# The experts' output bias: summed by TensorE at the end of layer 1 in place of by GpSimd in the middle of it

## The chip, the cores and the metric

The kernel runs on one core of one Trainium2 chip. The metric is the device time of one launch in microseconds (us); the median of three runs of the kernel before is 626.78 us (620.87 to 627.47). The five engines of the core run their own instruction queues and meet only at semaphores: TensorE (PE in the profile, with its weight loads as PEld), VectorE (DVE), ScalarE (ACT), GpSimd (POOL) and SyncE (SP, which here only issues transfers).

## The reference, cut to what matters

The input has 16 batches of 256 rows of 128 numbers. The network has an attention layer with 16 heads, then a layer with a second attention (4 heads) and a mixture of 8 experts. Each row goes to the one expert with the highest logit:

```python
idx = jnp.argmax(logits, axis=-1)
for e in range(E):                                   # E = 8, D = 128, DF = 512
    m = (idx == e)[:, None].astype(xf.dtype)
    h = jax.nn.relu(xf @ W1[e] + b1[e])
    out = out + m * (h @ W2[e] + b2[e])
```

The kernel uses relu(a + b1) = max(a, -b1) + b1. So it computes h' = max(x W1[e], -b1[e]) per row, and what is missing, b1[e] W2[e] + b2[e], is a constant row of 128 numbers per expert. These 8 rows, 1024 numbers in all, are **the output bias**, and it depends on the parameters alone. This is the part of the computation that the change moves.

## The kernel before, in words

There are three stages, each one a block of the program that ends with a barrier of all engines: the first layer (`first_layer`, about 0 to 337 us of the profiled span), the second attention with the sorting of rows by expert (`second_attention`, to about 504 us), and the experts (`experts`, to the end). All of it is float32, which TensorE takes as two records per matmul in the profile.

**Layer 1** is a loop over the batches, `iteration(i)` for i up to LAST + 2 = 17, written out by hand on each engine. In iteration i, TensorE makes the scores of batch i (line 226, into `psB`), the scores of batch i + 1 whose row maxima are needed (line 209, into the three banks of `psA`), the products of probabilities and values (`attend`, line 240) and the projections (lines 183 and 191). VectorE reduces each bank of `psA` to its maxima (line 331) and gives it back; the next scores into this bank wait for that (`a_free`). Between these it normalises the heads of the batch before (lines 346, 353 and 355; line 355 multiplies two operands that both lie in SBUF). ScalarE does the exponentials (line 493). GpSimd has per iteration: normalising a batch three ahead (lines 561 to 579), adding the attention's result two behind (lines 561 to 598), and spreading the keys of two ahead (`spread`, line 586, waiting for ScalarE's `kraw`). In iteration 16 only the end of the last batch is left: `attend(15, 3)`, then `project(15)` on TensorE, then VectorE's residual (lines 317 to 305) and GpSimd's `add_attention` (line 598), which raises `x1_ok`. On that, SyncE moves the last batch to `xs` (line 674) and ScalarE writes it to the output (line 535, counted by `kept`); SyncE waits for all moves to `xs` and for `kept` before it goes to the barrier.

**The output bias before.** From iteration 7, after `spread`, GpSimd also does `bias_part(f)` for f = 0 to 3 (line 617: slice f of W2 times the column of b1, 128x1024 numbers, summed over partitions only later), from iteration 8 `bias_sum(f)` (line 626: adds the product to `w["bias"]`), and in iteration 11 `bias_rest` (lines 631 to 633: adds b2 to partition 0, makes -b1 as `nb1T` and a tile of ones). In the experts' stage the matmul in `output` (line 1456) with `ones` as the stationary operand sums `w["bias"]` over the partitions and starts the sum of each tile.

The weights of the experts (`loads`) are fetched on ScalarE's queue in iterations 1 to 5; all users wait on `loaded`.

Of the kernel before, what the change touches and what calls it, by code (L numbers as in the profile page):

```python
# [8 lines left out]
ALU = mybir.AluOpType  # L9
ACT = mybir.ActivationFunctionType  # L10
AX = mybir.AxisListType

P = 128
B1, L1 = 16, 256
# [8 lines left out]
LAST = B1 - 1  # L23
# [8 lines left out]
def first_layer(nc, x, w_qkv, b_qkv, w_o, b_o, ident, identh, minus_half, xs, out, kept, loads2, loaded2, w, loads,  # L32
                loaded):

    with ExitStack() as ctx:
# [6 lines left out]
        def sem(name):  # L42
# [39 lines left out]
        psA = pb("psA", [P, 3, 512])  # L82
# [5 lines left out]
                 "m_step", "w_ok", "stats0", "stats1", "aggr0", "aggr1", "ln0_step", "ln1_step", "xn_ok", "xnb_ok",  # L88
                 "full", "free", "q_ok", "k_ok", "km_ok", "v_ok", "v_zero", "a_full", "a_free",
                 "turned", "norm_ok", "heads_ok", "onT_ok", "mrow0", "mrow1", "b_full", "b_free", "av_done", "o_ev", "rden_ok", "x1_ok", "stored",  # L90
                 "part_ok", "bias_ok"]
        S = {n: sem(n) for n in names}

        x_t = x.rearrange("b (p c) d -> p b c d", p=P)
# [53 lines left out]
        def _(pe):  # L148
            T = nc.tensor
# [95 lines left out]
            def project(b):  # L245
                pe.wait_ge(S["onT_ok"], b + 1)
                begin("out", b)
                token_major(onT, 1)

            def iteration(i):  # L250
                here, next_, done = fits(i, 0), fits(i, 1), fits(i, -1)
                for g in range(8):
                    if next_:
                        scores_for_max(i + 1, 2 * g)
                        scores_for_max(i + 1, 2 * g + 1)
                    if here and next_:
                        scores(i, 2 * g)
                        scores(i, 2 * g + 1)
                    if here and not next_ and g % 2 == 0:
                        for h in range(2 * g, 2 * g + 4):  # L260
                            scores(i, h)
                    if here and g in (3, 5, 7):
                        attend(i, g // 2 - 1)
                    if g == 0 and i >= 2 and here:
                        prep_v(i)
                    if g == 1 and done:
                        attend(i - 1, 3)
                    if g == 1 and fits(i, 2):
                        prep_x(i + 2)
                    if g in (2, 4) and fits(i, 2):  # L270
                        prep_qk(i + 2, g // 2 - 1, 0)
                        prep_qk(i + 2, g // 2 - 1, 1)
                    if g == 6 and done:
                        project(i - 1)

            pe.wait_ge(S["w_ok"], 5)
            prep_x(0)
# [154 lines left out]
        def _(act):  # L432
# [96 lines left out]
            for i in range(LAST + 2):  # L529
                if 1 <= i <= 5:  # L530
                    for to, source in loads[2 * i - 2:2 * i]:
                        act.dma_start(to, source, allow_slow_non_contiguous=True).then_inc(loaded, 16)
                iteration(i)
            act.wait_ge(S["x1_ok"], B1)
            act.dma_start(out[LAST * L1:B1 * L1, :].rearrange("(p c) d -> p c d", p=P),
                          x_all[:, 2 * LAST:2 * B1, :]).then_inc(kept, 16)
# [3 lines left out]
        def _(pool):  # L540
# [66 lines left out]
                if fits(i, 2):  # L607
                    spread(i + 2)

            b1_of = w["b1T"][:, :].rearrange("p (e f) -> p e f", f=NF)  # L610

            def bias_part(f):

                to = w["part"] if f else w["bias"]
                pool.wait_ge(loaded, 16 * len(loads))
                pool.wait_ge(S["bias_ok"], f)
                G.tensor_tensor(to[:, :].rearrange("p (e d) -> p e d", d=P),
                                w["w2"][:, f, :].rearrange("p (e d) -> p e d", d=P),
                                b1_of[:, :, f:f + 1].broadcast_to([P, NE, P]), ALU.mult
                                ).then_inc(S["part_ok" if f else "bias_ok"], 1)  # L620

            def bias_sum(f):

                pool.wait_ge(S["part_ok"], f)
                pool.wait_ge(S["bias_ok"], f)
                G.tensor_tensor(w["bias"][:, :], w["bias"][:, :], w["part"][:, :], ALU.add).then_inc(S["bias_ok"], 1)

            def bias_rest():

                pool.wait_ge(S["bias_ok"], NF)  # L630
                G.tensor_tensor(w["bias"][0:1, :], w["bias"][0:1, :], w["b2r"][:, :], ALU.add)
                G.tensor_scalar(w["nb1T"][:, :], w["b1T"][:, :], -1.0, None, ALU.mult)
                G.memset(w["ones"][:, :], 1.0)

            norm_x(0)
            norm_x(1)
# [10 lines left out]
            G.tensor_copy(identh[:, :], ident[:, :])  # L647
            for i in range(LAST + 3):
                iteration(i)
                if 7 <= i < 7 + NF:  # L650
                    bias_part(i - 7)
                if 7 < i < 7 + NF:
                    bias_sum(i - 7)
                if i == 7 + NF:
                    bias_rest()


        @block.sync
# [704 lines left out]
def expert_weights(nc, ctx, w):  # L1363

    W1, b1, W2, b2, g2, be2 = w
    t = {"w1": [P, NE * DF], "w2": [P, NF, NE * P], "b2r": [1, NE * P], "g2r": [P, P], "be2r": [P, P],
         "nb1T": [P, NE * NF], "b1T": [P, NE * NF], "bias": [P, NE * P], "part": [P, NE * P], "ones": [P, P]}
    t = {name: ctx.enter_context(nc.sbuf_tensor("e_" + name, shape, F32)) for name, shape in t.items()}
    loads = [(t["w1"][:, :].rearrange("p (e f) -> p e f", f=DF), W1.rearrange("e d f -> d e f"))]
    loads += [(t["w2"][:, f, :].rearrange("p (e d) -> p e d", d=P),  # L1370
               W2[:, f * P:(f + 1) * P, :].rearrange("e p d -> p e d")) for f in range(NF)]
    loads += [(t["b1T"][:, :], b1.rearrange("e (f p) -> p (e f)", p=P)),
              (t["b2r"][:, :], b2.rearrange("(o e) d -> o (e d)", o=1)),
              (t["g2r"][:, :], g2.partition_broadcast(P)), (t["be2r"][:, :], be2.partition_broadcast(P))]
    return t, loads


def experts(nc, w, ident, kept, sorting, sent, padded, y_sorted, out):

    with ExitStack() as ctx:  # L1380
        def sb(name, shape, dt=F32):
# [2 lines left out]
        def pb(name):  # L1384
# [18 lines left out]

        names = ["consts", "t_full", "yT_ok", "own_ok", "h_full", "h_ok", "o_full", "z0_ok", "st0", "st1", "mv0",
                 "mv1", "sd0", "sd1", "inv0", "inv1", "rs0", "rs1", "z1_ok", "z2_step", "z2_ok", "w_ok"]
        names += [f"ys{r}" for r in range(RING)] + [f"put{r}" for r in range(WRING)]
        S = {n: ctx.enter_context(nc.semaphore("ex_" + n)) for n in names}

        w1_i, w2_i, b1_i, row_i = sorting

# [17 lines left out]
        @block.tensor  # L1428
        def _(pe):
            T = nc.tensor  # L1430

            def turn(t):
                pe.wait_ge(S[f"ys{t % RING}"], 16 * (t // RING + 1))
                if t >= 2:
                    pe.wait_ge(S["yT_ok"], t - 1)
                T.transpose(psT[t % 2][:, 0:P], ys[:, t % RING, 0:P], ident[:, :]).then_inc(S["t_full"], 1)

            def hidden(t):
                pe.wait_ge(S["yT_ok"], t + 1)
                pe.wait_ge(S["own_ok"], t + 1)  # L1440
                if t >= 2:
                    pe.wait_ge(S["h_ok"], t - 1)
                for f in range(NF):
                    last = T.matmul(psH[t % 2][:, f * P:(f + 1) * P], own[:, t % 3, f * P:(f + 1) * P],  # L1444
                                    yT[:, t % 3, :], start=True, stop=True)
                last.then_inc(S["h_full"], 1)

            def output(t):
                g = group(t)
                k = t - FIRST[g]  # L1450
                e = pe.value_load(w2_i[0:1, t:t + 1], min_val=0, max_val=(NE - 1) * P)
                pe.wait_ge(S["h_ok"], t + 1)
                if k == 0 and g >= 2:
                    pe.wait_ge(S["z0_ok"], g - 1)
                to = psO[g % 2][:, k * P:(k + 1) * P]
                T.matmul(to, w["ones"][:, :], w["bias"][:, bass.ds(e, P)], start=True, stop=False)
                for f in range(NF):
                    last = T.matmul(to, hT[:, t % 2, f, :], w["w2"][:, f, bass.ds(e, P)], start=False,  # L1458
                                    stop=(f == NF - 1))
                last.then_inc(S["o_full"], 1)  # L1460

            turn(0)
            turn(1)
            for t in range(NS + 1):
                if t < NS:
                    hidden(t)
                if t + 2 < NS:
                    turn(t + 2)
                if t >= 1:
                    output(t - 1)  # L1470
# [179 lines left out]
def build_program(nc, a, out):  # L1650
    with ExitStack() as ctx:
# [3 lines left out]
        xs = ctx.enter_context(nc.sbuf_tensor("xs", [P, NT, P], F32))  # L1655
        y_sorted = nc.dram_tensor("y_sorted", (LAST_ROW, YROW), F32).ap()
        kept = ctx.enter_context(nc.semaphore("kept"))
        loaded2 = ctx.enter_context(nc.semaphore("loaded2"))
        parameters, loads2 = attention_parameters(nc, ctx, [a[k] for k in ("Wqkv", "bqkv", "Wo", "bo", "g1", "be1",
                                                                           "Wg")])  # L1660
# [12 lines left out]
                   for name, n in (("w1_i", NS), ("w2_i", NS), ("b1_i", NS), ("row_i", NS))]  # L1673
# [4 lines left out]
        second_attention(nc, parameters, loaded2, loads2, ident, identh,  # L1678
                         minus_half, xs, y_all, logits, w, loaded, loads, y_sorted, slots, slot_i, base, sorting, sent, zeros,
                         pad_i, padded)  # L1680
        experts(nc, w, ident, kept, sorting, sent, padded, y_sorted, out)


# [21 lines left out]
```

## Time and profile before

| | |
|---|---|
| median of the runs shown | 626.78 us (626.78, 627.47, 620.87) |
| span of the profiled execution, first to last instruction | 624.8 us |
| its own device time | not given with the profile; the median lies 2.0 us above its span |
| PE busy | 524.8 us, 84% of the span |
| DVE busy | 448.6 us, 72% |
| ACT busy | 358.2 us, 57% |
| POOL busy | 314.3 us, 50% |
| one full iteration of layer 1, spread to spread | 16.93 us, three of them 18.40 to 19.98 |
| mean granted TensorE clock | 0.905 of full |

A share of busy time is a mean over three stages that have different limits. In layer 1 TensorE is busy nearly all the time, so the length of an iteration there says more than the shares: it is read from one `spread` (line 586) to the next.

### The profile page before, as it was taken

How to read it: one execution, taken by the hardware profiler on the slowest of the kernel's cores; microseconds unless marked ns; L12 is line 12 of the kernel's file. 1: busy time of each engine (PE TensorE's matmuls, PEld its weight loads, DVE VectorE, ACT ScalarE, POOL GpSimd, SP SyncE). 2: the span in 40 equal slices, each digit the busy share in tenths (PEclk: the TensorE clock that was granted, in tenths of full speed). 3: DMA queues.
4: the chain of work that ended last, by engine and by line, in shares of the span. 5: the costliest groups of instructions: out<-in, count | busy, mean ns of one | idle time of the engine just before them, and what ended most of it. 6: DMA issues, size and time to landing. Idle time of an engine off the chain costs nothing. (4 is left out here: it accounts for less than half of the span.)

```text
span 624.8 us, 15886 instructions
## 1 busy us (share of the span) xinstructions
PE 524.8 (84%) x5168; PEld 383.2 (61%) x5168; DVE 448.6 (72%) x1274; ACT 358.2 (57%) x969; POOL 314.3 (50%) x523
## 2 busy tenths in 40 slices
PE   2899999999999999999972899999957249999910
PEld 2576666666666565666641677677736249999910
DVE  2255878888888888888842789998685626888860
ACT  1214567676676656677560688876653025767760
POOL 5140244433445567422133638887884610477776
PEclk9999999999999988999995899997775559999965
DMA  4300523111011100101111000000001122244333
GB/s 98 87 2 2 170 71 38 24 23 20 19 20 19 21 19 3 20 19 20 20 36 34 35 2 2 2 3 10 20 31 38 59 77 68 34 60 64 32 33 31
DMA packets 38099, 21.62 MB, mean 35 GB/s; under 512 B 13433, under 2 KB 36353, under 8 KB 38018
## 3 DMA queue, kind: packets, MB, share of 16 engines
q1 hardware_dynamic: 18544, 10.65, 7.6%
q0 software_dynamic: 6640, 4.92, 5.6%
q10 hardware_dynamic: 12834, 5.04, 3.2%
q8 instruction: 43, 0.70, 0.5%
q14 instruction: 38, 0.31, 0.2%
HBM read 10.11 MB, written 8.12 MB: 29 GB/s over the span
## 5 line engine op out<-in xcount | busy, mean ns | idle before, releaser
L331 DVE TENSOR_REDUCE nmax<-psA 128x2 f32<-128x512 f32 x256 | 164.9, 685 | 63.7 <-PE psA L209 63.1
L493 ACT ACTIVATE pr<-psB 128x512 f32<-128x512 f32 x250 | 136.0, 595 | 95.1 <-PE psB L226 94.9
L209 PE MATMUL psA<-km,qp 24*128 24x256 f32 x768 | 128.9, 432 | 2.2 <-DVE nmax L331 1.7
L226 PE MATMUL psB<-q,km 26*128 26x256 f32 (+1 forms) x752 | 112.6, 416 | 0.2 <-DMA q<-mT 0.2
L209 PEld LDWEIGHTS psA<-km,qp 24*128 24x128 f32 x768 | 81.2, 200 | 34.8 <-DVE nmax L331 22.6
L1627 POOL DMA_INDIRECT out<-wz,ys x39 | 63.3, 1624 | 53.0 <-ACT wz L1582 44.1
L586 POOL TENSOR_TENSOR km<-kraw,rows_of 128x768 f32<-128x768 f32 x16 | 23.5, 1467 | 122.7 <-ACT kraw L468 115.1
L226 PEld LDWEIGHTS psB<-q,km 26*128 26x128 f32 (+1 forms) x752 | 70.0, 191 | 1.3 <-DMA q<-mT 0.6
L240 PE MATMUL psO<-pr,v 128*32 128x256 f32 x1024 | 70.3, 393 | 0.1
L1180 ACT ACTIVATE prob<-psS,nbias 128x128 f32<-128x128 f32 x128 | 45.6, 386 | 7.0 <-DVE nbias L998 7.0
L240 PEld LDWEIGHTS psO<-pr,v 128*32 128x32 f32 x1024 | 27.2, 111 | 33.8 <-issue 22.5
L1483 DVE TENSOR_TENSOR hT<-psH,e_nb1T 128x512 f32<-128x512 f32 x39 | 27.0, 692 | 25.3 <-PE psH L1444 17.8
L183 PE MATMUL misc<-xnT,wqk 128*128 128x256 f32 x128 | 40.5, 444 | 3.2 <-ACT xnT L442 1.9
L1444 PE MATMUL psH<-yT,own 128*128 128x128 f32 x312 | 42.9, 282 | 0.0
L209 PE MATMUL psA<-kraw,qp 8*128 8x256 f32 x256 | 42.7, 416 | 0.0
L1296 POOL DMA_INDIRECT y_sorted<-y_all,slot_i x32 | 32.4, 1014 | 17.7 <-DVE slot_i L1047 9.9
L1458 PE MATMUL psO<-e_w,hT 128*128 x312 | 41.2, 275 | 0.0
L1444 PEld LDWEIGHTS psH<-yT,own 128*128 128x128 f32 x312 | 39.7, 199 | 0.0
L1458 PEld LDWEIGHTS psO<-e_w,hT 128*128 128x128 f32 x312 | 38.0, 192 | 0.0
L1565 ACT ACTIVATE own<-e_w 128x512 f32 x39 | 24.3, 623 | 23.5 <-PEq L752 18.1
L226 PE MATMUL psB<-q,kraw 27*128 27x256 f32 x248 | 36.0, 400 | 0.0
L183 PEld LDWEIGHTS misc<-xnT,wqk 128*128 128x128 f32 x128 | 24.2, 210 | 18.0 <-ACTq L452 6.8
(201 smaller groups left out, 1113.5 us busy)
## 6 DMA issues: line engine op xcount, KB each, us to landing
q<-mT SPq DMA_DIRECT2D x256, 1.0 KB
ys<-y_sorted SPq DMA_DIRECT2D x39, 72.0 KB, 1.9
e_w<-W ACTq DMA_DIRECT2D x1, 2048.0 KB
e_w<-W ACTq DMA_DIRECT2D x4, 512.0 KB
xs<-x_all SPq DMA_DIRECT2D x16, 128.0 KB
out<-x_all SPq DMA_DIRECT2D x15, 128.0 KB, 3.8
x_all<-x SPq DMA_DIRECT2D x1, 1536.0 KB, 8.9
out<-wz,ys POOLq DMA_INDIRECT x39, 3.3
```

What stands on the lines that cost most here:

```text
L183: made = T.matmul(misc[:, t * L1:(t + 1) * L1], wqk[:, k, t, :], xnT[:, b % 2, :], start=True, stop=True)
L209: last = T.matmul(psA[:, (16 * b + n) % 3, c * L1:(c + 1) * L1], query_part(b, h, depth, c), keys(b, h, depth, slice(0, L1)), start=True, ...
L226: last = T.matmul(bank_of(b, h)[:, c * L1:(c + 1) * L1], keys(b, h, depth, slice(c * P, (c + 1) * P)), queries(b, h, depth, slice(0, L1)), ...
L240: last = T.matmul(psO[32 * j:32 * j + 32, (quad % 2) * L1:(quad % 2 + 1) * L1], v32[:, b % SLOTS, c, 4 * quad + j, :], pr[:, (4 * quad + j ...
L331: V.tensor_reduce(nmax[:, b % 2, hf, :, at], psA[:, (16 * b + n) % 3, :].rearrange("p (c m) -> p c m", c=2), AX.X, ALU.max, negate=True).t ...
L493: A.activation(pr[:, h % PRING, :, :].rearrange("p c l -> p (c l)"), bank_of(b, h), ACT.Exp, scale=SCALE1).then_inc(S["b_free"], 1)
L1180: A.activation(prob[:, n, c, h, :], psS[s][:, u * P:(u + 1) * P], ACT.Exp, bias=nbias[:, s, u:u + 1], scale=SCALE2, accum_out=den[:, n, c, ...
L1296: G.indirect_dma_start(y_sorted, bass.IndirectOffsetOnAxis(slot_i[:, j:j + 1], 0), y_all[:, j, :], None).then_inc(sent, 16)
L1444: last = T.matmul(psH[t % 2][:, f * P:(f + 1) * P], own[:, t % 3, f * P:(f + 1) * P], yT[:, t % 3, :], start=True, stop=True)
L1458: last = T.matmul(to, hT[:, t % 2, f, :], w["w2"][:, f, bass.ds(e, P)], start=False, stop=(f == NF - 1))
L1483: V.tensor_tensor(hT[:, t % 2, :, :], psH[t % 2][:, :].rearrange("p (f n) -> p f n", f=NF), w["nb1T"][:, bass.ds(e, NF)].unsqueeze(2).broa ...
L1627: G.indirect_dma_start(out, bass.IndirectOffsetOnAxis(ids[:, t % RING, P:P + 1], 0), wz[:, t % WRING, :], None, compute_op=ALU.add).then_i ...
```

## The change

The products and sums on GpSimd are taken out; `expert_constants`, in iteration 7, keeps -b1 and the ones. TensorE makes the bias in iteration 16 of layer 1, in two groups of four experts, into two banks of `psA`, which by then no one else uses. The first group stands in its queue between `attend(15, 3)` and `project(15)`, the second behind `project(15)`. Each group is one matmul with one row (ones times b2, 512 columns) and 16 matmuls of 128 columns whose stationary operand is one column of b1, repeated 128 times, and whose moving operand is a slice of W2. So each of the 128 partitions of the result holds the whole bias row. ScalarE copies the two banks to `w["bias"]`, ahead of its wait for `x1_ok` and the last output. In the experts' stage the matmul that starts a tile's sum has the identity in place of the ones as the stationary operand. The tile `part` goes, and the eight semaphores `put` are made before the stages in place of within the last one.

```diff
+            def expert_bias(j):
+                pe.wait_ge(loaded, 16 * len(loads))
+                pe.wait_ge(S["ones_ok"], 1)
+                pe.wait_ge(S["a_free"], 16 * B1)
+                half = NE // 2
+                T.matmul(psA[:, j, :], w["ones"][0:1, :], w["b2r"][0:1, j * half * P:(j + 1) * half * P], start=True,
+                         stop=False)
+                for k in range(half):
+                    e = j * half + k
+                    for f in range(NF):
+                        last = T.matmul(psA[:, j, k * P:(k + 1) * P],
+                                        w["b1T"][:, e * NF + f:e * NF + f + 1].broadcast_to([P, P]),
+                                        w["w2"][:, f, e * P:(e + 1) * P], start=False,
+                                        stop=(k == half - 1 and f == NF - 1))
+                last.then_inc(S["bias_full"], 1)
...
                     if g == 6 and done:
                         project(i - 1)
+                    if i == LAST + 1 and g in (1, 6):
+                        expert_bias(g // 6)
...
                 iteration(i)
+            for j in range(2):
+                act.wait_ge(S["bias_full"], j + 1)
+                A.activation(w["bias"][:, j * 512:(j + 1) * 512], psA[:, j, :], ACT.Copy)
             act.wait_ge(S["x1_ok"], B1)
             act.dma_start(out[LAST * L1:B1 * L1, :].rearrange("(p c) d -> p c d", p=P),
...
-            def bias_part(f):
-                to = w["part"] if f else w["bias"]
...
-                G.tensor_tensor(to[:, :].rearrange("p (e d) -> p e d", d=P),
-                                w["w2"][:, f, :].rearrange("p (e d) -> p e d", d=P),
-                                b1_of[:, :, f:f + 1].broadcast_to([P, NE, P]), ALU.mult
-                                ).then_inc(S["part_ok" if f else "bias_ok"], 1)
-            def bias_sum(f):
...
-                G.tensor_tensor(w["bias"][:, :], w["bias"][:, :], w["part"][:, :], ALU.add).then_inc(S["bias_ok"], 1)
-            def bias_rest():
-                pool.wait_ge(S["bias_ok"], NF)
-                G.tensor_tensor(w["bias"][0:1, :], w["bias"][0:1, :], w["b2r"][:, :], ALU.add)
+            def expert_constants():
+                pool.wait_ge(loaded, 16 * len(loads))
                 G.tensor_scalar(w["nb1T"][:, :], w["b1T"][:, :], -1.0, None, ALU.mult)
-                G.memset(w["ones"][:, :], 1.0)
+                G.memset(w["ones"][:, :], 1.0).then_inc(S["ones_ok"], 1)
...
                 iteration(i)
-                if 7 <= i < 7 + NF:
-                    bias_part(i - 7)
-                if 7 < i < 7 + NF:
-                    bias_sum(i - 7)
-                if i == 7 + NF:
-                    bias_rest()
+                if i == 7:
+                    expert_constants()
...
-                T.matmul(to, w["ones"][:, :], w["bias"][:, bass.ds(e, P)], start=True, stop=False)
+                T.matmul(to, ident[:, :], w["bias"][:, bass.ds(e, P)], start=True, stop=False)
```

## Rows read from the trace of the kernel before

**Rows 1.** The page: its first line.
```profile
span 624.8 us, 15886 instructions
```

**Rows 2.** Windows from spread to spread: length, busy PE PEld DVE ACT POOL, clock, DMA.
```profile
182.13:199.06 16.93, 16.91 (x214) 10.71 (x210) 13.99 (x30) 11.87 (x25) 8.95 (x14) 1.00 0.10 19
199.06:217.46 18.40, 17.99 (x214) 11.32 (x210) 15.87 (x30) 11.87 (x25) 11.19 (x15) 1.00 0.09 18
217.46:237.41 19.95, 19.54 (x214) 12.05 (x210) 15.98 (x30) 11.87 (x25) 11.19 (x16) 0.91 0.08 15
237.41:257.39 19.98, 19.57 (x214) 11.87 (x210) 15.97 (x30) 11.87 (x25) 11.18 (x16) 0.91 0.08 16
257.39:274.32 16.93, 16.91 (x214) 10.71 (x210) 13.99 (x30) 11.87 (x25) 9.84 (x16) 1.00 0.10 19
```

**Rows 3.** POOL's sums: least/median/most ns, first to last start; then timeline: start, us.
```profile
L626 POOL TENSOR_TENSOR e_bias<-e_bias,e_part x3: 2360/2360/2364, 202.5 to 240.8; 128x1024 f32<-128x1024 f32 x3
...
258.81 2.33 POOL L631 TENSOR_TENSOR e_bias<-e_bias,e_b2r 1x1024 f32<-1x1024 f32 x1
261.13 0.43 POOL L632 TENSOR_SCALAR e_nb1T<-e_b1T 128x32 f32<-128x32 f32 x1
261.52 0.20 POOL L633 MEMSET e_ones<- 128x128 f32 x1
```

**Rows 4.** DVE's line 355, the same way; then the first and last long one.
```profile
L355 DVE TENSOR_TENSOR on<-oT,rden x32: 291/293/2207, 66.0 to 326.4; 128x128 f32<-128x128 f32 x32
...
202.78 2.21 DVE L355 TENSOR_TENSOR on<-oT,rden 128x128 f32<-128x128 f32 x1
...
241.13 2.21 DVE L355 TENSOR_TENSOR on<-oT,rden 128x128 f32<-128x128 f32 x1
```

**Rows 5.** Timeline over the end of layer 1; in brackets idle before and releaser.
```profile
322.50 0.71 PE L191 MATMUL misc<-wvo,onT 128*128 128x128 f32 x4
323.14 2.20 PE L240 MATMUL psO<-pr,v 128*32 128x256 f32 x32
...
327.93 1.01 PE L191 MATMUL misc<-wvo,onT 128*128 128x128 f32 x4 [2.59 <-ACT onT L487]
328.98 0.42 DVE L317 TENSOR_TENSOR r<-misc,xnb_all 128x256 f32<-128x256 f32 x1 [1.64 <-PE misc L191]
...
333.28 0.60 SPq L674 DMA_DIRECT2D xs<-x_all  x1
333.28 0.36 ACTq L535 DMA_DIRECT2D out<-x_all  x1
```

**Rows 6.** SP's wait at the barrier, and when it passed.
```profile
SPq L35 <- DMA xs<-x_all: 2.4, 1, 2.4
...
L35 SPq COMPARE_BRANCH  x1: 38/38/38, 337.5 to 337.5; - x1
```

**Rows 7.** The page's DMA issues: the last output, us to landing at the end.
```profile
out<-x_all ACTq DMA_DIRECT2D x1, 128.0 KB, 1.7
```

**Rows 8.** Timeline of PE in the experts' stage: four matmuls, and what follows.
```profile
522.12 1.06 PE L1444 MATMUL psH<-yT,own 128*128 128x128 f32 x8
523.02 0.27 PE L1436 MATMUL psT<-ident,ys 128*128 128x128 f32 x1
```

**Rows 9.** Timeline of PE at the start of layer 2.
```profile
342.25 2.07 PE L870 MATMUL psQK<-xy,uT 128*128 128x256 f32 x4 [0.47 <-ACT xy L1218]
344.11 1.06 PE L878 MATMUL psVO<-uT,xy 128*128 128x128 f32 x4
...
345.97 1.13 PE L870 MATMUL psQK<-xy,uT 128*128 128x256 f32 x4 [0.47 <-ACT xy L1218]
```

**Rows 10.** Timeline of ACT: a copy of 128x512 numbers from PSUM.
```profile
339.30 0.60 ACT L1172 ACTIVATE uT<-psS 128x512 f32<-128x512 f32 x1 [11.42 <-PE psS L849]
```

**Rows 11.** Windows, PE alone: length, busy (records), granted clock, DMA share, GB/s.
```profile
327.00:328.20 1.20, 0.27 (x2) 1.00 0.00 0
328.20:337.00 8.80, 0.74 (x4) 0.50 0.27 60
```

More of the change, by code:

```diff
@@ L90, in first_layer @@
                  "turned", "norm_ok", "heads_ok", "onT_ok", "mrow0", "mrow1", "b_full", "b_free", "av_done", "o_ev", "rden_ok", "x1_ok", "stored",
-                 "part_ok", "bias_ok"]
+                 "bias_full", "ones_ok"]
         S = {n: sem(n) for n in names}
@@ L608, in iteration @@
                     spread(i + 2)
-            b1_of = w["b1T"][:, :].rearrange("p (e f) -> p e f", f=NF)
-            def bias_part(f):
-                to = w["part"] if f else w["bias"]
+            def expert_constants():
                 pool.wait_ge(loaded, 16 * len(loads))
-                pool.wait_ge(S["bias_ok"], f)
-                G.tensor_tensor(to[:, :].rearrange("p (e d) -> p e d", d=P),
-                                w["w2"][:, f, :].rearrange("p (e d) -> p e d", d=P),
-                                b1_of[:, :, f:f + 1].broadcast_to([P, NE, P]), ALU.mult
-                                ).then_inc(S["part_ok" if f else "bias_ok"], 1)
-            def bias_sum(f):
-                pool.wait_ge(S["part_ok"], f)
-                pool.wait_ge(S["bias_ok"], f)
-                G.tensor_tensor(w["bias"][:, :], w["bias"][:, :], w["part"][:, :], ALU.add).then_inc(S["bias_ok"], 1)
-            def bias_rest():
-                pool.wait_ge(S["bias_ok"], NF)
-                G.tensor_tensor(w["bias"][0:1, :], w["bias"][0:1, :], w["b2r"][:, :], ALU.add)
                 G.tensor_scalar(w["nb1T"][:, :], w["b1T"][:, :], -1.0, None, ALU.mult)
-                G.memset(w["ones"][:, :], 1.0)
+                G.memset(w["ones"][:, :], 1.0).then_inc(S["ones_ok"], 1)
             norm_x(0)
@@ L1366, in expert_weights @@
     t = {"w1": [P, NE * DF], "w2": [P, NF, NE * P], "b2r": [1, NE * P], "g2r": [P, P], "be2r": [P, P],
-         "nb1T": [P, NE * NF], "b1T": [P, NE * NF], "bias": [P, NE * P], "part": [P, NE * P], "ones": [P, P]}
+         "nb1T": [P, NE * NF], "b1T": [P, NE * NF], "bias": [P, NE * P], "ones": [P, P]}
     t = {name: ctx.enter_context(nc.sbuf_tensor("e_" + name, shape, F32)) for name, shape in t.items()}
@@ L1375, in expert_weights, with experts @@
     return t, loads
-def experts(nc, w, ident, kept, sorting, sent, padded, y_sorted, out):
+def experts(nc, w, ident, kept, sorting, sent, padded, y_sorted, out, puts):
     with ExitStack() as ctx:
@@ L1405, in experts @@
                  "mv1", "sd0", "sd1", "inv0", "inv1", "rs0", "rs1", "z1_ok", "z2_step", "z2_ok", "w_ok"]
-        names += [f"ys{r}" for r in range(RING)] + [f"put{r}" for r in range(WRING)]
+        names += [f"ys{r}" for r in range(RING)]
         S = {n: ctx.enter_context(nc.semaphore("ex_" + n)) for n in names}
+        S |= {f"put{r}": puts[r] for r in range(WRING)}
         w1_i, w2_i, b1_i, row_i = sorting
@@ L1657, in build_program @@
         kept = ctx.enter_context(nc.semaphore("kept"))
+        puts = [ctx.enter_context(nc.semaphore(f"put{r}")) for r in range(WRING)]
         loaded2 = ctx.enter_context(nc.semaphore("loaded2"))
@@ L1680, in build_program @@
                          pad_i, padded)
-        experts(nc, w, ident, kept, sorting, sent, padded, y_sorted, out)
+        experts(nc, w, ident, kept, sorting, sent, padded, y_sorted, out, puts)
 def kernel(L0_attn_x, L0_attn_w_qkv, L0_attn_b_qkv, L0_attn_w_o, L0_attn_b_o, L0_ffn_Wqkv, L0_ffn_bqkv, L0_ffn_Wo,
```

## The prediction

> **What bounds the kernel now.** The first views, the page's span of 624.8 us [rows 1] and its busy shares, mislead here: GpSimd is the least busy of the four computing engines and TensorE the busiest, so taking work from the one and giving it to the other looks like a loss. But a share is a mean over three stages, and the change lies in layer 1 alone. So I read that stage iteration by iteration, in windows from one spread of the keys to the next [rows 2]. A plain iteration takes 16.93 us, with TensorE busy for 16.91 of them: TensorE is the bound there, and whatever makes it wait adds to the time. Three iterations take 18.40, 19.95 and 19.98 us with the same 214 TensorE records. They are the three in which GpSimd makes a running sum of the bias (three sums of 2.36 us, from 202.48 to 240.8 [rows 3]).
>
> The timeline says how. VectorE's product of heads and reciprocals, line 355, has a median of 0.29 us over 32 and a longest of 2.21 us [rows 4]. Three are that long, the first at 202.78, the last at 241.13: each starts 0.3 us into a sum (202.5 and 240.8 [rows 3]) and ends about 0.15 us behind its end. So three times VectorE stands for 1.92 us behind GpSimd. The row maxima of the next scores come late, and TensorE, which needs their PSUM bank back, waits: it is busy for 17.99 of the 18.40 us [rows 2]. The first such iteration loses 1.47 us (1.92 less 0.45 that was slack). The other two lose 3.02 and 3.05: there the granted clock of TensorE was 0.91 over the iteration against 1.00 in the others [rows 2], that is, after the pause it went for some us to the lower of its two levels (1.2 in place of 2.4 GHz), which is the further 1.55 to 1.58.
>
> **What is removed.** The three sums: 1.47 + 3.02 + 3.05 = 7.54 us on the path. The products cost nothing: the first of them, in the iteration from 182.13, and the last part, the addition of b2 (2.33 us at 258.81 [rows 3]), stand in iterations of 16.93 us [rows 2]. Taking them away gives nothing.
>
> **What stays on GpSimd.** The negated b1 and the ones, 0.43 + 0.20 = 0.63 us [rows 3], move to iteration 7. The work behind them there, the normalising of a batch three ahead, starts 0.63 us later than in a plain iteration and may touch line 355 for a moment; the first 0.45 us of such a touch was slack above. I cost it at 0. Without that slack it is 0.5 us once.
>
> **What is added at the end of layer 1.** The path there [rows 5]: the last attend (the second half of the 32 records from 323.14) ends at about 325.3; VectorE and ScalarE turn its result; the last projection runs at 327.93 for 1.01 us; the residual follows at 328.98; the two last transfers are issued at 333.28. SyncE passes its wait for the move to `xs` at 337.5 and with that the barrier opens [rows 6]. The last output, issued by ScalarE at the same moment, has landed 1.7 us later, at 335.0 [rows 7], so that branch has 2.5 us to spare.
>
> TensorE idles from 325.3 to 327.93, and the first bias group goes in there. Let T be the time of a group: 16 matmuls of 128 columns and one of 512, which I count as 4 more, so 20. For one of 128 columns I take the experts' stage, where four with a new stationary operand each take from 522.12 to 523.02, 0.89 us, or 0.2225 each [rows 8]: it is the nearest row, a stream of the same shape. T = 20 x 0.2225 = 4.45 us. The projection then starts at 325.3 + 4.45 = 329.75, 1.82 late; but it follows busy TensorE, and at the full clock the same four records take 0.71, not 1.01 [rows 5], so what hangs on it is late by 1.82 - 0.30 = 1.5 us. The move to `xs` and the barrier are late by as much.
>
> The second group runs behind the projection, from 330.4 to 334.85. ScalarE copies the first bank in its idle time and the second, 0.60 us [rows 10], to 335.5; only then comes its wait for the last batch (now 334.8) and the last output, which lands 1.7 later, at 337.2. The move to `xs` lands at 337.5 + 1.5 = 339.0. So the second group and the copies cost nothing as long as that cover of 1.8 us holds; each us of T above it counts twice on this branch.
>
> Bounds of T. No row shows a stationary operand that is one column repeated. Below: 4.45 as taken; a lower end would need a faster stream than any row has. Above, at the full clock: the projection's four records, loads not hidden, take 0.64 to the next (322.50 to 323.14 [rows 5]), 0.32 a matmul, T = 6.4: the projection is late by 3.5, the last output would land at 341.05 and `xs` at 341.0, so the end is late by 3.5. At the lower clock: two matmuls of 256 columns take 342.25 to 344.11 [rows 9], 0.465 per 128 columns, T = 9.3.
>
> **Edits at nothing.** Identity for ones in the experts' stage: same shape, same records. No DMA is added or moved except the last output, above. TensorE's new waits (weights loaded, ones made, `psA` free) are met long before 325. The tile taken out and the place of the semaphores move addresses only.
>
> **The sum.** Span 624.8 [rows 1] - 7.54 + 1.5 = 618.7. The profile doesn't give its own device time; the median of 626.78 lies 2.0 above its span, and with the same 2.0 I get **620.7 us**, 6.1 or 1.0% below.
>
> **Rivals.**
>
> *Slow groups, full clock* (T = 6.4): end late by 3.5, so 622.7. For it: the projection's own rows; against: the experts' stream hides its loads [rows 8].
>
> *Layer 2 starts at the higher clock.* Before, TensorE goes to the lower level at 328.2, after 1.2 us with 0.27 busy [rows 11], and stays there past the barrier, to about 345: of two equal pairs of line 870 the first takes 2.07 us, the second 1.13 [rows 9, 11]. With the groups it is busy to 334.85. If the higher level lasts into layer 2, its first steps shrink: that pair by 0.94, the other few, by my estimate from it, together about as much, so 1.9 us less: 618.8. Against it: the idle stretch to the barrier is still some 4 us, longer than the one after which the clock fell before. The Trainium skill (TensorE: Matmul & The Clock Gate, Part 1) calls the lower clock the default and says activity releases it; by that the new matmuls hold the clock in their own stretch, and the idle stretch behind them takes it away again.
>
> *The work was hidden anyway.* GpSimd is off the chain, its sums stay without effect on the time, and the long iterations have another cause. Then the change only adds its 1.5: 628.3. Against it: three sums, three long products, three long iterations, at the same times. The Trainium skill (Perfetto Trace Analysis, Identifying the Most-Contended Engine) says to improve the engine with the highest occupancy; by that the change helps the wrong engine and burdens the right one. The rows go against it in this stage.
>
> *The second group holds the last output.* If the matmuls run at the lower clock (T = 9.3), the projection starts at 334.6, the second group ends at 344.8, the copy at 345.4, and the last output lands at 347.1: the end is 9.6 late, more than the 7.54 won, and the time is 628.9. It decides from 325.3 + 2T + 0.7 + 0.6 + 1.7 = 337.5 + 7.54 on, T = 8.4. Against it: the clock is full at 327 to 328.2 [rows 11], and TensorE now works there.
>
> **How the numbers follow.** Forecast 0.57, slow groups 0.18, higher clock in layer 2 0.12, hidden anyway 0.04, second group 0.04, others 0.05. About 1% (6.3 us, below 620.5) is what can be told from no change, and my forecast lies at that bound: half of its chance (how often the clock falls after a pause may differ from one execution to the next, and two falls are worth 3.1 us of the 7.54), nearly all of the higher clock and little else make faster 0.42; slower by over 1% needs a T of 11.5 or something I have not seen, 0.03; within 0.55. The range takes in the higher clock and the slow groups, each with some 2 to 3 us for the scatter of the runs shown (6.6 us from lowest to highest): 616 to 625.
>
> **What would show it.** Line 355 never above some 0.6 us; the iterations from 199 on all 16.9; granted clock 1.00 to the end of layer 1; a group of 17 matmuls in 4.4 to 4.5 us from 325.3 - 7.5 on, the projection right behind it; SyncE still released by the move to `xs`, not by the last output. I am wrong if another product of VectorE stands as long behind GpSimd, if a group takes over 6.4 us, or if ScalarE's copy ends after the last batch by more than 2.5 us.

## The result and the profile after

The changed kernel takes 621.29 us (median of 20 runs, 619.92 to 625.67) against 626.73 for the kernel before in the same rounds (20 runs, 620.87 to 629.04). The ratio is 0.9936, 95% interval 0.9918 to 0.9954: 0.6% faster, or 4.0 us by the ratio (the means lie 4.1 us apart, the medians 5.4), where 6.1 us were forecast. In its profiled execution the span is 621.5 us and the device time 623.28, so what lies around the span is 1.8 us here. Over its 20 runs it is 1.7 to 3.1 us, with a mean of 2.2; in 33 runs of the kernel before it is 1.7 to 1.8 each time. So some 0.45 us of what the change gives is lost around the span, where no profile looks.

The first view is again the windows from spread to spread, now of the kernel after, iterations 7 to 10 (length, busy PE, PEld, DVE, ACT, POOL, granted clock, DMA):

```profile
181.58:198.52 16.94, 16.92 (x214) 10.71 (x210) 14.00 (x30) 11.89 (x25) 7.55 (x16) 1.00 0.10 19
198.52:215.45 16.93, 16.91 (x214) 10.71 (x210) 14.00 (x30) 11.90 (x25) 6.98 (x14) 1.00 0.10 19
215.45:232.38 16.93, 16.91 (x214) 10.71 (x210) 13.99 (x30) 11.89 (x25) 6.98 (x13) 1.00 0.09 18
232.38:249.31 16.93, 16.91 (x214) 10.71 (x210) 13.99 (x30) 11.89 (x25) 6.98 (x13) 1.00 0.10 19
```

The three long iterations [rows 2] are gone and the clock is full in each. The product of VectorE (line 355 before, line 374 now; shortest, median and longest in ns):

```profile
L374 DVE TENSOR_TENSOR on<-oT,rden x32: 291/293/615, 66.0 to 318.4; 128x128 f32<-128x128 f32 x32
```

Its longest is 0.62 us in place of 2.21 [rows 4]. Now the end of layer 1, TensorE's timeline (start, duration, line) with ScalarE's row that makes the projection's input, which answers to [rows 5]:

```profile
315.06 2.21 PE L240 MATMUL psO<-pr,v 128*32 128x256 f32 x32
317.19 1.12 PE L256 MATMUL psA<-e_b2r,e_ones 1*128 1x512 f32 x2
318.24 3.84 PE L261 MATMUL psA<-e_w,e_b1T 128*128 128x128 f32 x32
319.29 0.51 ACT L506 ACTIVATE onT<-onR,b_cols 128x256 f32<-128x256 f32 x1 [3.16 <-DVE onR L383]
321.92 0.61 PE L191 MATMUL misc<-wvo,onT 128*128 128x128 f32 x4
322.46 1.12 PE L256 MATMUL psA<-e_b2r,e_ones 1*128 1x512 f32 x2
```

The first group runs from 317.19 to the projection at 321.92, 4.7 us; the projection's input was made by 319.8, so it starts 2.1 us late. SyncE's waits there, and the page's row of the last output (us to landing at its end), against [rows 6, 7]:

```profile
SPq L713 <- DMA out<-x_all: 3.8, 1, 3.8
SPq L35 <- PEq L35: 0.2, 1, 0.2
```
```profile
out<-x_all ACTq DMA_DIRECT2D x1, 128.0 KB, 3.9
```

This is new: SyncE now waits for the last output, which takes 3.9 us to land in place of 1.7.

All kernels have the same layers 2 and 3 but for one operand, so I cut each profile at three points: the start of the spread of iteration 8, the first matmul of layer 2, and the first copy of the experts' stage. The first stretch holds the three sums and the end of layer 1; how long layer 1 takes to get there is left out (197.3 to 200.9 us in the profiles of this document, the nine more sums apart, with no order among the kernels).

| | iteration 8 to layer 2 | layer 2 | experts | span |
|---|---|---|---|---|
| before | 138.86 | 167.42 | 119.44 | 624.8 |
| after | 133.28 | 170.62 | 119.12 | 621.5 |

Layer 1 gives 5.6 us in these two profiles, and layer 2 takes 3.2 us of it back. Whether the change does that, and how much of the 7.54 us is there in other executions, is what the experiments are for.

### The profile page after: what moved, and what is told of

Same layout as the page of the kernel before. It is cut to its first block and busy times, and to the rows that moved or that the text cites. A ratio compares the mean times of both kernels' runs of the same rounds, so it can differ in the third digit from the quotient of the medians.

```text
span 621.5 us, 16011 instructions
## 1 busy us (share of the span) xinstructions
PE 529.1 (85%) x5236; PEld 389.6 (63%) x5236; DVE 441.6 (71%) x1274; ACT 360.3 (58%) x971; POOL 298.0 (48%) x515
## 3 DMA queue, kind: packets, MB, share of 16 engines
q0 software_dynamic: 6640, 4.92, 5.6%
## 5 line engine op out<-in xcount | busy, mean ns | idle before, releaser
L209 PE MATMUL psA<-km,qp 24*128 24x256 f32 x768 | 124.5, 427 | 1.0 <-POOL km L608 0.5
L226 PE MATMUL psB<-q,km 26*128 26x256 f32 (+1 forms) x752 | 111.0, 411 | 0.0
L209 PEld LDWEIGHTS psA<-km,qp 24*128 24x128 f32 x768 | 79.2, 198 | 32.1 <-DVE nmax L350 20.5
L240 PE MATMUL psO<-pr,v 128*32 128x256 f32 x1024 | 68.8, 386 | 0.1
L583 POOL TENSOR_SCALAR ve<-mv_r 128x2 f32<-128x2 f32 x16 | 3.8, 237 | 76.2 <-DVE mv_r L324 76.2
```

Source lines behind the costliest of these rows:

```text
L209: last = T.matmul(psA[:, (16 * b + n) % 3, c * L1:(c + 1) * L1], query_part(b, h, depth, c), keys(b, h, depth, slice(0, L1)), start=True, ...
L226: last = T.matmul(bank_of(b, h)[:, c * L1:(c + 1) * L1], keys(b, h, depth, slice(c * P, (c + 1) * P)), queries(b, h, depth, slice(0, L1)), ...
L240: last = T.matmul(psO[32 * j:32 * j + 32, (quad % 2) * L1:(quad % 2 + 1) * L1], v32[:, b % SLOTS, c, 4 * quad + j, :], pr[:, (4 * quad + j ...
```

## The experiments

In what follows a stall is an iteration in which line 355 stands behind a sum, and a fall is TensorE's clock going to its lower level after it. My theory: VectorE's product stands behind GpSimd's sum because both read SBUF; each stall costs 1.47 us, and the clock's falls and layer 2's length go with the execution. Rivals: the amount of GpSimd's work is what delays layer 1; the falls belong to the stall; the bias matmuls cost layer 2 something.

**The sums later in GpSimd's queue.** The kernel before, with `bias_sum` taken from behind the spread and put into the next iteration:

```diff
                     add_bo(i + 3)
+                if 8 < i < 8 + NF:
+                    bias_sum(i - 8)
                 if fits(i, -2):
...
-                if 7 < i < 7 + NF:
-                    bias_sum(i - 7)
```

> The kernel before with the same sums on GpSimd, only later in its queue: each sum stands between adding the output bias of the attention (line 579 of before) and add_attention of the next iteration, where no product of line 355 falls. Theory (the sum holds VectorE's two-input product up): line 355 stays at 0.3 to 0.6 us, every iteration from 131 us on takes 16.93 us, layer 1 ends about 7.5 us earlier than in the profile of before (first matmul of layer 2 at 330.4), with nothing to pay at its end; the time is 1 to 2 us below the changed kernel. Rival (GpSimd's amount of work is what delays layer 1): GpSimd has the same work, the three iterations stay at 18.4 to 20 us and the time stays at that of before.

619.26 us (6 runs, ratio 0.989, interval 0.9857 to 0.9923). Its windows of the same three iterations:

```profile
199.90:216.83 16.93, 16.91 (x214) 10.71 (x210) 13.99 (x30) 11.87 (x25) 11.27 (x15) 1.00 0.10 19
216.83:233.77 16.94, 16.92 (x214) 10.71 (x210) 14.00 (x30) 11.87 (x25) 11.27 (x16) 1.00 0.10 18
233.77:250.70 16.93, 16.91 (x214) 10.71 (x210) 13.99 (x30) 11.87 (x25) 11.26 (x15) 1.00 0.10 19
```

GpSimd is as busy as before (11.27 against 11.19 us [rows 2]), and the stall is gone. The place of the sums was the cause, not the amount of work. Nothing is paid at the end: 131.03 us from iteration 8 to layer 2. (Layer 2 starts at 330.93 and not at 330.4, since iteration 8 starts 0.84 us later than in the first profile of before.)

**The changed kernel again**, unchanged.

> The changed kernel unchanged. In its first profile layer 1 was 6.1 us shorter than before (first matmul of layer 2 at 331.8 against 337.9), but layer 2 (to the first copy of the experts' stage) took 170.6 us against 167.4. Theory: the length of layer 2 goes with where TensorE's clock falls in one execution and not with the change, so this profile gives some other length, within 166 to 172; layer 1 again ends at 331.8 +- 0.3. Rival (the bias matmuls cost layer 2 its clock at the start): 170 to 171 again, with the second pair of 256-column matmuls in layer 2 still slow.

622.07 us (12 runs, ratio 0.994, 0.9918 to 0.9962). From iteration 8 to layer 2 133.24 us, as in the first profile; layer 2 167.32 in place of 170.62. So those 3.2 us belonged to that execution. (Layer 2 starts at 332.52, outside the 331.8 +- 0.3 that I had expected, since iteration 8 starts 0.76 us later here.) The first matmuls of layer 2 in this profile show where the clock was:

```profile
332.52 0.63 PE L847 MATMUL psS<-ident,u_nat 128*128 128x128 f32 x4 [4.41 <-PEq L35]
...
336.85 2.07 PE L869 MATMUL psQK<-xy,uT 128*128 128x256 f32 x4 [0.47 <-ACT xy L1217]
...
340.68 1.13 PE L869 MATMUL psQK<-xy,uT 128*128 128x256 f32 x4 [0.47 <-ACT xy L1217]
```

The transposes take 0.63 us (1.08 in the first profile of after), at the higher level (granted clock 1.00); the first pair of line 869 is back at the lower one (0.50), as in [rows 9].

**The kernel before again**, unchanged, twice.

> The kernel before unchanged. Theory: in each execution the three products wait 1.92 us, but the clock falls after only some of the pauses, so layer 1 ends between 334.8 (no fall) and 339.5 (three); layer 2 between 166 and 172. Rival (the clock falls are part of the stall): 337.9 again with the two falls at the same places, and layer 2 at 167.4.

> The kernel before, a third profile, to count falls of the clock: so far two, one and none... of three pauses fell (two in the first profile, one in the second; one of twelve with more sums). Theory (the falls go with the execution): between none and three of the three iterations at 20 us, the others at 18.4. Rival (two of three as a rule): 19.9 to 20 us twice.

625.19 and 628.15 us, one run each. Their windows of the three iterations, the second profile and then the third:

```profile
199.32:219.36 20.04, 19.62 (x214) 12.06 (x210) 15.99 (x30) 11.88 (x25) 11.22 (x15) 0.91 0.09 16
219.36:237.77 18.41, 17.99 (x214) 11.32 (x210) 15.89 (x30) 11.89 (x25) 11.22 (x16) 1.00 0.09 17
237.77:256.18 18.41, 17.99 (x214) 11.32 (x210) 15.89 (x30) 11.88 (x25) 11.21 (x15) 1.00 0.09 17
```
```profile
199.78:218.18 18.40, 17.99 (x214) 11.32 (x210) 15.88 (x30) 11.88 (x25) 11.20 (x15) 1.00 0.09 18
218.18:236.58 18.40, 17.99 (x214) 11.32 (x210) 15.88 (x30) 11.88 (x25) 11.21 (x15) 1.00 0.09 16
236.58:258.07 21.49, 21.08 (x214) 12.91 (x210) 15.97 (x30) 11.99 (x25) 11.21 (x16) 0.84 0.08 15
```

An iteration without a fall takes 18.40 each time. The falls come at other places: in the first of the three, then in the last (and there for longer, 4.56 us over 16.93, which neither theory had). In three profiles the stalls cost 7.54, 6.07 and 7.50 us. Layer 2 took 167.06 and 168.50.

**A memset for the sum.** It leaves the three sums of the bias out.

```diff
-                G.tensor_tensor(w["bias"][:, :], w["bias"][:, :], w["part"][:, :], ALU.add).then_inc(S["bias_ok"], 1)
+                G.memset(w["blank"][:, :], 0.0).then_inc(S["bias_ok"], 1)
...
```

> The kernel before with each of the three sums replaced by one memset of 128x2688 numbers in the same place of GpSimd's queue, about as long (2.4 us); it leaves the sums of the bias out. Theory in its narrow form (the two compete for reading SBUF): a memset reads nothing, line 355 stays at 0.29 us and the iterations at 16.93, layer 1 ends at about 330.4. Rival (any GpSimd instruction of that length at that moment holds VectorE): line 355 at 2.2 us, iterations of 18.4 to 20 us.

619.85 us, one run; 131.29 us from iteration 8 to layer 2. GpSimd's memset and VectorE's product at the place of the first stall, on each engine's timeline:

```profile
202.48 2.34 POOL L626 MEMSET e_blank<- 128x2688 f32 x1
```
```profile
202.80 0.29 DVE L355 TENSOR_TENSOR on<-oT,rden 128x128 f32<-128x128 f32 x1
```

The same start, the same length, and the product isn't touched. So it is what GpSimd does, not that it is busy: the sum reads two tiles in SBUF, the memset only writes one. The trace lists no wait of line 355 in either kernel, so the engines do not meet only at semaphores, as was said at the start: here GpSimd held VectorE up with none between them. The Trainium skill (SBUF — State Buffer, Who interferes with whom) states this rule: a VectorE instruction with two SBUF inputs contends with a GpSimd instruction that reads SBUF, not with one that only writes it. This run agrees: 2.21 us with the sum, 0.29 with the memset.

**The sum in four pieces.**

```diff
-                G.tensor_tensor(w["bias"][:, :], w["bias"][:, :], w["part"][:, :], ALU.add).then_inc(S["bias_ok"], 1)
+                for c in range(0, NE * P, 2 * P):
+                    last = G.tensor_tensor(w["bias"][:, c:c + 2 * P], w["bias"][:, c:c + 2 * P],
+                                           w["part"][:, c:c + 2 * P], ALU.add)
+                last.then_inc(S["bias_ok"], 1)
```

> The kernel before with each of the three sums cut into four instructions of 256 columns (0.72 us each by line 598 of before, the same shape), at the same place. Theory (VectorE's product stands behind the one GpSimd instruction that runs, and gets in ahead of the next): line 355 takes at most 0.29 + 0.7 = 1.0 us, and as the first 0.45 us of a delay is slack the three iterations lose 0 to 0.3 us each: layer 1 ends at 330.4 to 331.3. Rival (the stall lasts for the whole of GpSimd's work): 2.2 us or more and 18.4 us per iteration.

Line 355 in this kernel, then the sum and the product at the first place:

```profile
L355 DVE TENSOR_TENSOR on<-oT,rden x32: 291/293/614, 65.9 to 320.7; 128x128 f32<-128x128 f32 x32
...
204.29 2.84 POOL L627 TENSOR_TENSOR e_bias<-e_bias,e_part 128x256 f32<-128x256 f32 x4
...
204.59 0.57 DVE L355 TENSOR_TENSOR on<-oT,rden 128x128 f32<-128x128 f32 x1
```

At the three places it takes 0.57 us and the iterations take 16.93 to 16.94: it stands behind one piece of GpSimd's 2.84 us and gets in before the next. 131.04 us from iteration 8 to layer 2. The one run took 623.01 us; its span holds a start up to iteration 8 that is 1.8 us longer than in the first profile of before, and a layer 2 of 169.78.

**Nine more sums.** The kernel before with, in iterations 1 to 7, 12 and 13, a memset as a place holder (not in 7) and one more sum of unused tiles behind it.

```diff
+                if 1 <= i <= 7 or 12 <= i <= 13:
+                    if i != 7:
+                        G.memset(w["blank"][:, :], 0.0)
+                    G.tensor_tensor(w["again"][:, 0:NE * P], w["again"][:, NE * P:2 * NE * P], w["again"][:, 2 * NE * P:],
+                                    ALU.add)
...
```

> The kernel before with nine more sums of the same size on GpSimd (of tiles that no one uses), in iterations 1 to 7, 12 and 13, each placed as the three are (behind a memset where the product stood, so that it meets line 355): twelve pauses in all. Theory (each pause costs 1.47 us, and the clock falls after only some of them, 1.57 us more): twelve iterations of 18.4 or of about 20 us, both kinds among them, some three to eight long ones, 638 to 652 us. Rival (the fall belongs to the pause, and the first one is spared by its place): nearly all at 20 us, 650 us or more.

638.16 us, one run. All twelve products take 2.06 to 2.21 us. From spread to spread ten of these iterations take 18.25 to 18.41 us (the twelfth has no spread behind it, and the clock was full in it); the clock fell in one, the last of these three windows:

```profile
209.16:227.57 18.41, 18.00 (x214) 11.32 (x210) 15.88 (x30) 11.88 (x25) 11.21 (x15) 1.00 0.09 17
227.57:245.98 18.41, 18.00 (x214) 11.33 (x210) 15.88 (x30) 11.88 (x25) 11.22 (x15) 1.00 0.08 16
245.98:265.99 20.01, 19.60 (x214) 12.10 (x210) 15.97 (x30) 11.88 (x25) 11.21 (x16) 0.91 0.08 16
```

I had expected three to eight falls. The cost of a stall holds (1.32 to 1.48 us); how often the clock falls after one, I can't forecast: 4 of 9 in the three profiles of before, 1 of 12 here.

**The changed kernel without the groups and the copies.**

```diff
-                    if i == LAST + 1 and g in (1, 6):
-                        expert_bias(g // 6)
...
-            for j in range(2):
-                act.wait_ge(S["bias_full"], j + 1)
-                A.activation(w["bias"][:, j * 512:(j + 1) * 512], psA[:, j, :], ACT.Copy)
...
+                G.memset(w["bias"][:, :], 0.0)
```

> The changed kernel without TensorE's two bias groups and without ScalarE's two copies (the bias is left out, a memset stands for it). Theory (the first group holds up the last projection, the second is covered): from the spread of iteration 8 (line 608 of the changed kernel, 198.5 in its profile) to the first matmul of layer 2 it takes 131.3 us, as in before without its stalls, against 133.3 with the groups: the groups cost 2.0 us. Rival (the groups cost nothing and something else lengthens the end): 133.3 again.

619.28 us, one run; 131.09 us from iteration 8 to layer 2 against 133.28 and 133.24. The groups cost 2.2 us.

**The groups cut otherwise.** Ahead of the projection only what fits into TensorE's wait for it; the matmuls are the same, and those of the first group go on behind it (`CUT` is 6 of the 16).

```diff
+                if j == 0:
+                    expert_products(0, 0, CUT)
+                else:
+                    expert_products(0, CUT, half * NF)
+                    expert_products(1, 0, half * NF)
...
```

> The changed kernel with the same 34 matmuls, cut otherwise: ahead of the last projection only the matmul of one row and 6 of the 16 of the first group (1.05 + 6 x 0.22 = 2.4 us, which fits into the 2.6 us in which TensorE waits for the projection's input), all the others behind the projection. Theory (only the delay of the projection is on the path): the projection starts when its input is there, the rest of the groups ends some 6.9 us behind it, the last output lands about when the move to xs does, and from the spread of iteration 8 to layer 2 it takes 131.3 to 131.8 us instead of 133.3; the time is 1.5 to 2 us below the changed kernel. Rival (the path runs over the copies and the last output): the end is as late as before this cut or later, 133.3 or more.

619.86 us (8 runs, ratio 0.9914, 0.9884 to 0.9944). TensorE's end of layer 1:

```profile
317.07 1.12 PE L257 MATMUL psA<-e_b2r,e_ones 1*128 1x512 f32 x2
318.13 1.60 PE L271 MATMUL psA<-e_w,e_b1T 128*128 128x128 f32 x12
319.74 0.71 PE L192 MATMUL misc<-wvo,onT 128*128 128x128 f32 x4
320.38 1.12 PE L257 MATMUL psA<-e_b2r,e_ones 1*128 1x512 f32 x2
321.44 6.07 PE L271 MATMUL psA<-e_w,e_b1T 128*128 128x128 f32 x52
329.82 0.63 PE L857 MATMUL psS<-ident,u_nat 128*128 128x128 f32 x4 [2.31 <-PEq L36]
```

SyncE's wait before the barrier:

```profile
SPq L723 <- DMA out<-x_all: 3.9, 1, 3.9
```

The projection starts at 319.74, when its input is there, and though the other matmuls run on to 327.5, layer 2 starts at 329.82: 131.48 us from iteration 8. Of the groups' 2.2 us the delay of the projection was 1.8. The 0.4 left lie on the other branch here: the last output is issued behind the second copy, at 327.55, and SyncE waits for it last. By the ratios this kernel is 1.4 to 1.6 us below the changed one, as expected, but the intervals overlap.

**The last output first.** The changed kernel, with ScalarE's output issued between its two copies.

```diff
-            for j in range(2):
+            def bias_in(j):
...
+            bias_in(0)
             act.wait_ge(S["x1_ok"], B1)
             act.dma_start(out[LAST * L1:B1 * L1, :].rearrange("(p c) d -> p c d", p=P),
                           x_all[:, 2 * LAST:2 * B1, :]).then_inc(kept, 16)
+            bias_in(1)
```

> The changed kernel with ScalarE's last output issued ahead of the second copy, so at the same moment as the move to xs, as in before (in the changed kernel it comes 0.5 us behind that move, takes 3.9 us to land in place of 1.7 and is what SyncE waits for last). Theory (its packets run into those of the move to xs): it lands in 1.7 us again, SyncE waits for the move to xs, and from the spread of iteration 8 to layer 2 it takes 133.0 us, 0.3 less than the 133.3 of the changed kernel. Rival (the landing time of this transfer is chance): 3.9 us again, 133.3.

620.14 us, one run. The output lands in 1.7 us again and SyncE waits for the move to `xs`:

```profile
SPq L35 <- DMA xs<-x_all: 2.6, 1, 2.6
```

So the 3.9 us (3.8 in the second profile of after) come from being issued 0.5 us behind that move. But the stretch takes 133.16 us: 0.1 less, not the 0.3 expected, since the move to `xs` lands right behind.

**The sums later, once more**, beside the cut groups.

> The kernel with the sums later in GpSimd's queue, run again beside e6: below the kernel before by 1.1% (0.986 to 0.992), iterations all 16.93 us, from the spread of iteration 8 to layer 2 131.0 to 131.3 us, so level with e6 within 1 us.

618.94 us (6 runs, ratio 0.9902, 0.9868 to 0.9937). The stretch was 131.70, 0.4 more than expected: in this execution the clock had gone to the lower level already before the projection (granted clock 0.50 from 319.0 to 319.6), which took 1.22 us. This version and the cut groups are level. Beside the changed kernel, in the same rounds, the sums later had 619.26 us against 622.07; the intervals of the two ratios overlap at their ends, 0.989 (up to 0.9923) and 0.994 (down to 0.9918). The means of these runs lie 2.8 us apart, 2.35 of it in the span and the rest around it, where the sums later have 1.7 to 1.8 us in all 12 runs, as the kernel before has. Among the kernels that compute the whole bias the sums later have the lowest medians, and they are the smallest edit; nothing sets them apart from the cut groups.

## Why the prediction was right, and where its sizes were off

- **What bounds the stage** held: iterations of 16.93 us, any wait of TensorE is paid. The rival that GpSimd's work was hidden fell with the profile of after; the sums later and the memset show by what: the sum's place, and that it is a sum, which reads SBUF, and not a memset.
- **What is removed, 7.54 us**: right for the execution profiled. As a forecast for the median it was mis-sized: 4.41 of it (three times 1.47) is there in each profile of before, the rest hangs on the clock's falls. Three profiles of before give 7.54, 6.07 and 7.50, mean 7.0; one with twelve stalls had a single fall. I had put this into the chances and not into the number. The sums later take the stalls away and add nothing, so their runs price them over whole executions: 6.8 and 6.6 us by the means (626.0 less 619.2, and 625.4 less 618.8), each known to some 2 us.
- **Constants on GpSimd at 0**: right, iteration 7 takes 16.94 us.
- **T = 4.45 us**: it is 4.7. The 16 matmuls of 128 columns take 0.22 each, as taken from the experts' stage; a stationary operand that is one column repeated costs nothing more. The one of 512 columns takes 1.05, not 0.89, and 0.1 goes by before the projection's first matmul. Neither slow groups nor the lower clock came.
- **The end 1.5 us late**: 2.0 against the stretch with the memset (133.28 less 131.29), 2.2 against the kernel without groups. The projection's delay is 1.7 to 1.9 of it, since T was longer. The rest is a step that failed: "the second group and the copies cost nothing as long as that cover of 1.8 us holds". It took a landing of 1.7 us for the last output; issued behind the move to `xs` it needs 3.9, and this used up the cover. SyncE was released by the last output; I had named its release by the move as one of the signs that would show the forecast. The price is small: from the issue of the move to layer 2 it takes 4.92 and 4.87 us in the two profiles of after, and 4.63 to 4.80 in the ten profiles in which the output is issued together with the move, so 0.1 to 0.3 us.
- **The same 2.0 us around the span**: a term that I carried over unchanged. It is 1.7 to 1.8 us in the kernel before and 2.2 in the mean of the changed kernel's 20 runs (2.2 again in the 12 runs of its repetition), so 0.45 us more. The cut groups have 1.7 to 2.6 in 8 runs, mean 1.9; the sums later, without the groups, none above 1.8.
- **Layer 2 at the higher clock**: only its very first matmuls, in one of the two profiles of after (0.63 against 1.08 us). Worth nothing that can be seen in its length.
- **The sum, and some luck.** By the means, with the stalls as the sums later price them: 626.0 - 6.8 + 2.2 + 0.45 = 621.9, against a mean of 621.9. The three sizes that were off all erred the same way, which is why 4.0 us came and not 6.1; the scatter of the runs would allow a us or two either way. That the median of 621.29 lies only 0.6 us above the forecast of 620.7 is in part luck: the median of before lies 0.7 above its mean, that of after 0.6 below its own.
- **What stays open**: why more time lies around the span when TensorE makes the bias, how often the clock falls after a stall, and the scatter of layer 2. That took 167.1 to 168.5 us in the four profiles of kernels with the stalls (mean 167.6) and 166.9 to 170.6 in the nine without (mean 168.6). A us given back there is not needed for the sum, but the profiles overlap, and no run shows that there is none.

## What to carry to other kernels

When one engine's instruction is now and then several times its median, look at what another engine does in the same memory at that very time, even where no semaphore joins the two; moving or cutting the one that holds it up may do as well as taking it away, and here it cost no other engine anything. Before you price a stall with the clock's falls in it, count them in more than one profile: one shows only how many there were once, here two where the mean of three was 1.3. And when work is put into another engine's idle time, put in only as much as the idle time holds ahead of the next thing on the path.

## What the runs showed of the hardware that was not expected

A transfer of 128 KB issued at the same moment as another on a second queue landed in 1.7 us; issued 0.5 us behind it, in 3.9 and 3.8 us; 2.7 us behind it (the groups cut), in 1.7 again. And VectorE's product that stands behind GpSimd for a whole sum of 2.36 us is held for 0.3 us only when the same sum is four instructions, which GpSimd does back to back in 2.84 us: VectorE gets in between two of them.
